# Moving the query projections to the end of each slot in the shared PSUM banks of an attention stage

## The reference, cut to what matters

```python
Q = (queries @ Wq).reshape(b, nq, H, HD).transpose(0, 2, 1, 3) * ind_q[:, None, :, None]   # H, HD = 16, 64
scores = jnp.einsum('bhqd,bhkd->bhqk', Q, K) / jnp.sqrt(jnp.float32(HD))
attn = jax.nn.softmax(scores, axis=-1)
out = jnp.einsum('bhqk,bhkd->bhqd', attn, V)
out = out.transpose(0, 2, 1, 3).reshape(b, nq, H * HD)
return out @ Wo
```

## Time and profile before

| | |
|---|---|
| median of 3 runs | 1181.32 us (1177.41 to 1184.25) |
| the profiled execution, its own time | 1175.89 us |
| its span | 1174.0 us |
| second attention, from first `x` to last `out` | 646 to 1081 us of the span |
| busy over the span | TensorE 77%, VectorE 62%, GpSimd 55%, ScalarE 49% |

### The profile page before, as it was taken

The page is one execution under the profiler, slowest core; times in us unless marked ns, Lnnn a source line. Parts: engine busy times, 40 slices in busy tenths (PEclk is TensorE's granted clock), DMA queues, the critical chain, the costliest instruction groups (busy, mean ns, idle before and its releaser), DMA issues. The chain is left out here.

```text
span 1174.0 us, 28543 instructions
## 1 busy us (share of the span) xinstructions
PE 907.9 (77%) x10881; PEld 713.1 (61%) x10881; DVE 731.3 (62%) x1778; ACT 579.6 (49%) x954; POOL 644.9 (55%) x656
## 2 busy tenths in 40 slices
PE   2479888765567666299992589898889888898898
PEld 1357676542222222189992488887878887787565
DVE  3567777626577675156551557676867766664787
ACT  1147888756665757056662224343433433433564
POOL 1258898764777775344444644555546354521565
PEclk9998999967777887599996689999999999999999
DMA  6221222009557755777766404042432404001921
GB/s 165 79 75 58 65 79 74 8 9 291 221 192 222 287 212 202 267 200 202 201 184 225 172 22 171 20 169 68 157 95 96 167 20 165 19 3 27 193 70 36
DMA packets 107940, 152.29 MB, mean 130 GB/s; under 512 B 14101, under 2 KB 84674, under 8 KB 101410
## 3 DMA queue, kind: packets, MB, share of 16 engines
q1 hardware_dynamic: 73986, 116.91, 31.0%
q0 software_dynamic: 8480, 20.99, 5.8%
q10 hardware_dynamic: 25344, 12.59, 3.8%
HBM read 84.66 MB, written 65.54 MB: 128 GB/s over the span
## 5 line engine op out<-in xcount | busy, mean ns | idle before, releaser
L1477 POOL DMA_INDIRECT rows_x<-rows_r,index_r x128 | 137.6, 1075 | 68.6 <-issue 36.7
L923 POOL DMA_INDIRECT fetched_a<-rows_y,chosen_row x128 | 126.2, 986 | 82.7 <-DVE att_a L831 49.3
L450 POOL TENSOR_TENSOR p_lo_a<-probs_a,p_hi_a 128x1024 f16<-128x1024 f32 x64 | 136.1, 2132 | 40.2 <-ACT p_hi_a L313 40.0
L646 PE MATMUL psum<-v_x_a,probs_a 128*128 128x65 f32 x1024 | 125.0, 276 | 0.0
L646 PEld LDWEIGHTS psum<-v_x_a,probs_a 128*128 128x128 f32 x1024 | 120.9, 194 | 0.0
L734 ACT ACTIVATE q_a_a<-psum 128x512 f16<-128x512 f32 x64 | 38.2, 597 | 150.3 <-PE psum L666 142.7
L1680 POOL TENSOR_TENSOR h_lo_t<-hidden_t,h_hi_t 96x512 f16<-96x512 f32 x48 | 55.6, 1158 | 86.9 <-ACT h_hi_t L1630 86.9
L816 DVE TENSOR_REDUCE negmax_a<-psum 128x8 f32<-128x1024 f32 x64 | 78.2, 1222 | 30.0 <-remote 21.7
L696 PE MATMUL psum<-wo,att_t_a 128*128 128x128 f32 x512 | 67.3, 287 | 20.7 <-DVE q_b_a L802 18.8
L312 ACT ACTIVATE probs_a<-psum 128x1024 f32<-128x1024 f32 x64 | 65.7, 1027 | 30.0 <-PE psum L170 29.9
L359 DVE TENSOR_REDUCE negmax_a<-psum 128x8 f32<-128x1024 f32 x64 | 77.8, 1215 | 4.1 <-PE psum L186 3.9
(11 more groups left out here) (362 smaller groups left out, 3130.5 us busy)
## 6 DMA issues: line engine op xcount, KB each, us to landing
values<-v_out_r SPq DMA_DIRECT2D x16, 1040.0 KB
v_x_a<-values SPq DMA_DIRECT2D x16, 1040.0 KB, 7.7
keys<-k_out_r SPq DMA_DIRECT2D x16, 1024.0 KB
listed_t<-rows_x SPq DMA_DIRECT2D x96, 128.0 KB, 2.5
rows_y<-result_t ACTq DMA_DIRECT2D x48, 256.0 KB, 2.4
k_a_a<-keys SPq DMA_DIRECT2D x16, 512.0 KB
k_b_a<-keys SPq DMA_DIRECT2D x16, 512.0 KB
share_f<-shares SPq DMA_DIRECT2D x14, 512.0 KB, 8.1
```

The lines of the kernel that those rows point to most:

```text
L450: nc.gpsimd.tensor_tensor(p_lo[:, s % RING0, :], probs[:, s % NPR, :], p_hi[:, s % RING0, :], ALU.subtract).then_inc(s_plo, 1)
L646: last_ = nc.tensor.matmul(PV[:, part, i * (HD + 1):(i + 1) * (HD + 1)], probs[:, s % 3, lane(part, i)], v_x[:, par, b % GB, h, :], start= ...
L923: nc.gpsimd.indirect_dma_start(fetched[:, b % NF1, k, :], None, rows_y, bass.IndirectOffsetOnAxis(ap=chosen["row"][:, b, k:k + 1], axis=0) ...
L1477: nc.gpsimd.indirect_dma_start(rows_x, bass.IndirectOffsetOnAxis(ap=index[:, g * GB + t, k:k + 1], axis=0), rows[:, g % 2, t, :, :].rearra ...
```

## The change

Both query halves go to the end of their slot's list, behind `att` (and ahead of `y`, `l`, `m`). Half 1 stays in its even slot and moves from the head to the tail; half 0 stays in the tail of its odd slot and changes places with `att`. The expression gives, for even s, sequence (s+4)/2, half 1, and for odd s, sequence (s+5)/2, half 0, as before. All engines take the new order from the same function, and the banks are dealt out anew by `places1`.

```diff
     if s % 2 == 0:
         if 0 <= s - 4 < 2 * B:
             head.append(("out", (s - 4) // 2))
-        if 0 <= s + 4 < 2 * B:
-            head.append(("q", ((s + 4) // 2, 1)))
         if 0 <= s + 2 < 2 * B:
             tail.append(("nmt", (s + 2) // 2))
     elif 0 <= s + 5 < 2 * B:
         head.append(("x", (s + 5) // 2))
-        tail.append(("q", ((s + 5) // 2, 0)))
     if 0 <= s - 2 < 2 * B:
         tail.append(("att", s - 2))
+    if 0 <= s + 5 - (s + 1) % 2 < 2 * B:
+        tail.append(("q", ((s + 5) // 2, (s + 1) % 2)))
     for kind, lag in (("y", 13), ("l", 14), ("m", 17)):
```

## The result

The changed kernel takes 1209.13 us (median of 7 runs, 1198.43 to 1211.9), the kernel before 1179.54 (7 runs, 1176.01 to 1184.69) on the same chip: 1.0246 of before, 95% interval 1.0209 to 1.0283. That is 29.6 us slower. The prediction was 1178.0 with a range from 1167 to 1188, so time and sign were both missed. The profiled execution of the changed kernel is its fastest, 1198.43 us, 22.5 above the profiled one of before. What the other six lost beyond it, some 10 us, no trace shows. One run of all those in this document, of e3_xhat_first, fell in a slow state (1542.63 us at a granted clock of 0.56) and stands in no ratio.

A forecast was written before the change was run, and what follows sets the result against it. The prediction took TensorE as the fullest engine, busy 45.76 of 51.40 us in eight slots, its idle time mostly waits for VectorE's q_b. Its terms summed to -3.3 us, from the median 1181.3 to 1178.0, range 1167 to 1188.

The forecast's parts named there:

- x behind q1: Even-slot tails, order nmt, att, q1, x: q1's wait for nmt's copy is free, x loses 0.08 us each; +1.3 us.
- The clock: Slot 48: with out waiting only 0.1 us, the granted clock should stay up; -1.7 us.
- rival C: Slots with s mod 8 = 5: TensorE's waits bring the clock down six times; +6.5 us, 1187.8; chance 0.12.
- the wait of `x` for `q_b` in the slot behind `l`: x shares a bank with q1 and waits 1.1 us, where before it waited 0.30; +5.4 us over six.
- two clock gains: The clock staying up at slot 48, -1.7 us, and at the first plain out, another 1.6 us gained.
- Start of the stage: Slot 0: q1, formerly done during the wait for the first exponentials, comes behind it at half clock; +1.1 us.
- plain `out` slots: Outs of slots 4, 6, 8 and 10: out starts at 1.30 instead of 2.26, 0.95 us gained; -5.7 us in all.
- `xhat` wait: At six places, x of 13 to 53, x waits 1.1 us for GpSimd's xhat; +1.2 us in all.
- y: Mean wait of 1.28 us at y becomes 0.2 at y and 0.8 at out; -1.8 us over six.
- A (`xhat` in time): x does not wait 1.1 us for xhat at six places; -9.9 us, 1171.4; chance 0.22.
- B: All 28 waits go, about 1150; or half the l and grade charges and the xhat wait absent, 1167; chance 0.10.
- D: Scores wait 0.34 us for ScalarE's exponentials in each of 28 pairs of slots; +9.5 us, 1187.5; chance 0.06.

The follow-up runs named there:

- e3_xhat_first: The changed kernel with GpSimd's normal2 one slot later, right behind normal and ahead of the gathers; 0.9985 of before.
- e7: The changed kernel with GpSimd's gathers replaced by SyncE's plain loads of fixed rows, on a chip where before takes 1178.11 us; 1149.21 us.
- r1: The changed kernel run once more, unedited, on a chip where before takes 1141.83 us; 1.0069 of before.
- e2: The kernel before with only query half 1 moved to the tail behind att, half 0 staying ahead of att; 1.0102 of before.
- e4: The changed kernel with GpSimd's gathers replaced by SyncE's plain loads of fixed rows, on a chip where before takes 1141.57 us; 0.996 of before.
- e5: The kernel before with GpSimd's gathers replaced by SyncE's plain loads of fixed rows; 1132.1 us.
- e1: The kernel before with only query half 0 moved behind att, half 1 staying at the head of its even slot; 0.9969 of before.
- e6: The changed kernel with y, l and m ahead of the query half in the tail; 0.9919 of before.
- r3: The changed kernel run a third time, unedited, on a chip where before takes 1178.11 us; 1199.4 us.
- e8: The changed kernel with y, l and m ahead of the query half and normal2 one slot later, behind normal; 0.98 of before.
- e9: The kernel before with query half 0 behind att, y and m, half 1 left at the head, and normal2 behind normal; 0.987 of before.

## Why the prediction was wrong

**The step that failed first** is in *x behind q1*: "q1 waits for nmt's copy (...), which costs nothing as issue reaches it at 0.69." The 0.64 behind it came from a slot whose copy began 0.03 us after its matmul. Where the release is late, 1.71 us are paid there, and 9.9 us in six slots on chip A. Before the change `x` stood two places behind `nmt` and waited on the same copy, at the same distance. After 690 us it was never late there; in slot 42 the gather had ended by then. With `q1` gone from the head, the maxima's matmuls of slot 42 begin 4.62 us after `out` instead of 5.24, and the gather 4.19 after it instead of 3.76, and so they meet. So the failed step is a wait looked up in one slot of the old schedule and carried into the new one, whose gathers stand differently. In the eight slots from 40 to 48 on chip A every other interval held within some 0.2 us: `out` to `x` 6.70 us where the steps give 6.85, `x` to `x` 12.00 for 12.05, `x` to `out` 7.78 for 7.71 and 4.66 for 4.85. Only `out` of slot 42 to the `x` of 43 takes 8.09 for 6.33, and that is 1.76 more, the wait of the timeline above. These are the least disturbed eight slots of the stage: into slot 48 they have 12.56 us, where the other five cycles have 14.00 to 18.23.

**The second** is *The clock*, a term of -1.7 where chip C shows +7.6, and the weight of rival C, 0.12. Its price for a fall was right, 1.6 forecast and 1.52 measured. Its place was half right: on chip C the clock falls one item later in the cycle, behind the wait of `x` for `q_b` in the slot behind `l`, which the prediction itself priced at 1.1 us (1.04 measured) and did not carry into the clock. "Waits of 1.28 did not bring it down" is a true reading, but it does not say when a wait is harmless. Which waits bring the clock down is not settled by the runs. It is not their number or length alone: in slot 45 of the kernel before on chip A TensorE is idle for 0.99 and 1.28 us, ending at 961.13 and 963.24, and on chip C the kernel before waits 27 times for about 1 us, all without a fall. What the versions with falls on B and C, and e7, share is the wait of 1.0 us of the `x` behind `l` (r1 has five falls in six cycles, e2 four, e7 three, e3 and e4 two), and no version without it falls between 690 us and the last `out` (before on C, e5, e1, e6). With the same waits the clock falls in some cycles and not in others.

**The rest of the sum held in total, in part by luck.** The sum without its two clock gains (1.7 at slot 48 and 1.6 behind the `out` of slot 4), neither of which chip C offers, is -3.3 + 1.7 + 1.6 = 0.0 us. On chip C the stage is 6.9 longer, less 7.6 of clock: -0.7. But two misses cancel in it. *Start of the stage* was forecast to cost 1.1 us, with 1.2 gained at the first `out`; from the first `x` to that `out` the changed kernel is 2.2 us shorter on C (44.4 to 42.3) and 2.5 on A. The terms of the eight-slot cycles are worth 4.8 us on C, clock left out, where they add up to 3.0. By terms: plain `out` slots gain 0.82 each there (11.84 to 11.02) for 0.95; on chip A the four give 3.1 us for 5.7. The wait for `q_b` is left in 12 places at 0.8, 0.8 forecast. The `xhat` wait comes six times, 0.78 on C and 0.83 on A for 1.1. *y* was a miss in its kind: it was to gain from a wait of 1.28, which on chip C is 0.97, so the gain is absent. Eight slots without a fall take 49.48 us on C and 48.85 before, 0.63 more where the prediction had 0.4.

**So the 24.0 us of the stage on chip A** are 6.9 that chip C shows too and 17.1 that go with late releases. By slots, summed over the out-to-out intervals: into s mod 8 = 0, behind `l`, 2.98 more on average of six (18.23 at worst, where C has 12.56 without a fall); into 6, 0.72; into 2, 0.42; into 4, 0.96; the first four give back 3.1, and the start 2.5. Of the 17.1, 9.3 are idle time of TensorE and 7.9 busy time: idle time rises by 4.3 us on A (57.8 to 62.1) and falls by 5.0 on C (43.0 to 37.9), busy time rises by 19.8 on A and 11.9 on C. What one late release costs was not measured, since it also makes idle time behind which the clock falls. The new wait at line 663 is 9.9 us by itself.

**Rivals.** A (`xhat` in time) and B are refuted by the six waits. D did not occur: no wait for the exponentials is among the costly ones. C was right in its mechanism, and its 1187.8 was too low because late releases came on top. The sign of being wrong that the prediction gave for C, over 53 us with the clock under 1.0, is what came, with 59.00 and 0.91; but on chip A it was more than C.

**Left open**: what inside the chip holds a result back while GpSimd issues gathers, and why chips A and D do it and B and C do not. That it is tied to the gathers is shown by the pair r3 and e7, one profiled execution each, and by the first place of the stage. When it strikes is read from the traces and was not tried: in the changed kernel on A VectorE was already waiting at twelve maxima whose matmuls ended inside a gather with another one close behind, and all twelve were released 2.0 to 3.1 us late; at five others, inside a gather with none close behind, it took 0.04 to 1.4 us. On chip C the same two kernels have 0.04 to 0.05 us throughout.

## What to carry to other kernels

A release that a step treats as free must be looked up at every place where it occurs, not in one, and again in the new order: a row "remote" on an engine off the path is a price that the path pays once the schedule moves under it. Where items share banks in turn, it pays to put the ones with the longest release last and behind the rare items, so that nothing comes two places behind them within a slot (e6, e8). A new wait of about 1 us has to be priced with the clock too, here some 1.5 us for each fall, with a real chance and not as a remote rival; that waits of 1.3 us elsewhere in the old schedule did no harm is no proof that the new one will do none.

## What the runs showed of the hardware

The same kernel takes 1141.57 and 1141.83 us on chips B and C, and 1179.54 and 1178.11 on A and D (two chips, or one and the same), 3.3% apart (1179.54 / 1141.83 = 1.033). Of the 33.7 us between the spans on A and C (1174.0 and 1140.3) 23.7 lie in this stage, 432.3 against 408.6. The changed kernel's stage differs more, 456.3 against 415.5. A change that costs 0.7% on one chip thus costs 2.5% on another.

Late releases are seen by VectorE and ScalarE at the same moment, 961.48 and 961.51, and after 690 us up to 2.5 us late. TensorE itself is held in the same moments. In slot 45 of the kernel before it stands idle for 0.99 us, put down to issue, ending at 961.13, just ahead of the late release at 961.37, in the middle of twelve matmuls that are all recorded. This is no gap in the record: every trace has the same 5324 matmuls in the stage, and idle time put down to issue comes 23 times, 8.1 us in all, in the kernel before on A (17 times and 8.0 us in the changed one, 19 and 8.5 in r3, 18 and 5.9 in e8, 16 and 4.8 in e9), and not once on B or C or in e7. In the kernel before all seven late releases after 690 us have such a query half beside them, which takes 1.2 to 2.2 us from its first matmul to its last instead of 0.62. So while GpSimd issues gathers back to back on A and D, TensorE's own work is held up, and not only the engines that wait for its results. As the ends of matmuls in the traces are modelled, it stays open how much of a late release is the result coming late and how much is TensorE itself finishing late.
